# Gates of the last two up-projection batches on VectorE instead of TensorE

## The reference, cut to what matters

```python
x = x + xattn(layernorm(x), ctx)                  # (4, 512, 1024); stages a to c of the kernel
z = layernorm(x)                                  # stages d and e
logits = einsum('bsh,he->bse', z, gate_w)         # gate_w: (1024, 8)
routing_weights, _ = top_k(logits, 2)
h = relu(einsum('bsh,hi->bsi', z, up_w)) ** 2     # up_w: (1024, 2048)
shared_out = einsum('bsi,ih->bsh', h, down_w)
x_latent = einsum('bsh,hl->bsl', z, fc1_w)        # fc1_w: (1024, 512)
moe_out = (x_latent @ expert_w) * sum(routing_weights)
y = layernorm(shared_out + moe_out @ fc2_w, gamma, beta)
out = x + y
```

## Time and profile before

| | |
|---|---|
| median of 3 runs | 2098.47 us |
| the profiled execution | 2098.85 us |
| its span, first to last instruction | 2097.1 us |
| TensorE busy | 2076.1 us, 99% |
| VectorE, ScalarE, GpSimd busy | 805.5, 693.4, 754.7 us |
| mean granted TensorE clock | 0.997 |

### The profile page before, as it was taken

How to read it: one execution, slowest core, us unless ns; L and a number is a source line. 1 busy time by engine, 2 the same in 40 slices (tenths; PEclk the granted TensorE clock), 3 DMA queues, 4 the chain that set the end, 5 groups by cost and what they waited for, 6 DMA issues and landing times.

```text
span 2097.1 us, 30206 instructions
## 1 busy us (share of the span) xinstructions
PE 2076.1 (99%) x9532; PEld 1732.2 (83%) x9532; DVE 805.5 (38%) x1418; ACT 693.4 (33%) x1206; POOL 754.7 (36%) x616
## 2 busy tenths in 40 slices
PE   8999999999999999999999999999999999999998
PEld 7888888888888888888888878787878888888886
DVE  4221312178888888831121412313231332222223
ACT  5121111167777777741111223112123311111111
POOL 2533030147777777662112343010024422222221
PEclk9999999999999999999999999999999999999999
DMA  5743433635655655534347554252433622222222
GB/s 194 255 171 141 146 124 107 183 83 146 158 149 148 161 153 142 129 117 150 130 157 198 210 156 145 105 156 104 136 99 134 207 91 84 90 90 86 85 76 67
DMA packets 302750, 286.29 MB, mean 137 GB/s; under 512 B 146896, under 2 KB 214480, under 8 KB 301776
## 3 DMA queue, kind: packets, MB, share of 16 engines
q1 hardware_dynamic: 188128, 196.58, 29.9%
q10 hardware_dynamic: 114544, 88.76, 14.9%
HBM read 184.32 MB, written 100.68 MB: 136 GB/s over the span
## 4 chain that ended last, share of the span: by engine, by line
PE 97%; DVE 1%; ACT 1%; DMA 0%; issue 0%; POOL 0%; SPq 0%; DVEq 0%; POOLq 0%; ACTq 0%
PE psum L118 30%; PE psum L119 30%; PE psum L120 30%; PE psum L985 3%; PE psum L1031 1%; PE psum L1032 1%; PE psum L1012 1%; PE psum L1013 1%; PE psum L1697 0%; PE psum L1696 0%; DMA staging<-in_wqkv 0%; PE psum L232 0%; DVE small L181 0%; DMA staging<-in_ctx 0%; DVE operands L353 0%
## 5 line engine op out<-in xcount | busy, mean ns | idle before, releaser
L118 PE MATMUL psum<-operands 128*128 128x512 f32 (+3 forms) x2888 | 1113.7, 386 | 9.7 <-DVE operands L353 9.4
L119 PE MATMUL psum<-operands 128*128 128x512 f32 (+3 forms) x2888 | 1111.9, 385 | 0.0
L120 PE MATMUL psum<-operands 128*128 128x512 f32 (+3 forms) x2888 | 1109.2, 384 | 0.0
L118 PEld LDWEIGHTS psum<-operands 128*128 128x128 f32 (+1 forms) x2888 | 544.6, 189 | 109.0 <-DVE operands L353 9.3
L120 PEld LDWEIGHTS psum<-operands 128*128 128x128 f32 (+1 forms) x2888 | 545.0, 189 | 105.9
L119 PEld LDWEIGHTS psum<-operands 128*128 128x128 f32 (+1 forms) x2888 | 545.6, 189 | 94.6
L1276 POOL TENSOR_TENSOR operands<-staging,operands 128x512 fp32r<-128x512 f32 x92 | 118.7, 1301 | 349.8 <-ACT operands L1271 349.3
L1157 DVE TENSOR_REDUCE small<-psum 128x1 fp32r<-128x576 f32 x256 | 192.9, 754 | 89.8 <-PE psum L985 89.7
L1935 POOL TENSOR_TENSOR operands<-operands 128x640 fp32r<-128x640 f32 x64 | 100.8, 1577 | 319.1 <-ACT operands L1930 319.1
L905 POOL TENSOR_TENSOR operands<-staging,operands 128x512 fp32r<-128x512 f32 x128 | 164.5, 1293 | 34.4 <-ACT operands L1079 25.6
L1786 DVE TENSOR_TENSOR staging<-staging 128x512 f32<-128x512 f32 x64 | 46.6, 748 | 322.6 <-ACT staging L1744 321.8
(11 more groups left out here) (111 smaller groups left out, 1284.7 us busy)
## 6 DMA issues: line engine op xcount, KB each, us to landing
h_scratch<-staging ACTq DMA_DIRECT2D x80, 256.0 KB, 2.3
operands<-h_scratch SPq DMA_DIRECT2D x64, 320.0 KB, 3.1
operands<-recip_scratch SPq DMA_DIRECT2D x64, 192.0 KB, 4.3
o_scratch<-staging SPq DMA_DIRECT2D x64, 192.0 KB, 5.0
operands<-o_scratch SPq DMA_DIRECT2D x64, 192.0 KB, 2.8
operands<-q_hi_scratch ACTq DMA_DIRECT2D x14, 768.0 KB, 5.9
operands<-q_lo_scratch ACTq DMA_DIRECT2D x14, 768.0 KB, 6.2
staging<-in_x SPq DMA_DIRECT2D x20, 512.0 KB, 3.6
```

What stands on the lines that cost most here:

```text
L118: e.matmul(o, lh, rh, start=first, stop=False)
L119: e.matmul(o, lh, rl, start=False, stop=False)
L120: return e.matmul(o, ll, rh, start=False, stop=last)
```

## The change

The gates of batches 2 and 3 are made by VectorE, in the bodies of batches 1 and 2, while z lies in rows in `XN2`. A copy of the gate weights, transposed (8 experts x 1024), is put in memory as `g_d`. SP loads sixteen rows of 512 of it for each of the two batches, each spread over all 128 partitions, into two buffers that take the place of `GW` once TensorE's gates of batches 0 and 1 are done; twelve of these loads stand ahead of job f3's, four ahead of f0's. For each row VectorE issues four `tensor_tensor_reduce` (one for each tile of tokens): z's half row times the spread row into a PSUM bank that is free (one bank in group 0, two later), and the sum into one column of `g_acc`. Rows 0 to 2 stand after group 0, 3 to 7 after group 1, 8 to 12 after group 2, 13 to 15 after group 3, and then the copy of the sums and the two largest.

To have z early enough, the load of x1, the root and the norm of the next batch go to the front of the body, on ScalarE ahead of group 0's eviction and on VectorE ahead of group 0's squares; the store of z goes from group 2 to group 1. Jobs now stand ahead of the block loads, and after group 3 ScalarE waits for the copy of the sums before it loads blocks over z. TensorE's loop makes gates in batches 0 and 1 alone. VectorE's two middle bodies are written out instead of a loop.

```diff
+        def d_gate_row_in(e, b, i):
+            if i == 0:
+                e.wait_ge(*past(g_rl[0], 16))
+                e.sem_inc(idle, 1)
+                e.wait_ge(*past(d_gm, 2))
+                e.sem_inc(idle, 1)
+            e.wait_ge(*past(g_use, b * (ST * GR) + ST * (i - 1 - GR)))
+            e.sem_inc(idle, 1)
+            e.dma_start(raw(g_row[i % 2]), g_d[i * NB:(i + 1) * NB].partition_broadcast(P)).then_inc(g_rl[i % 2], 16)
+
+        def d_gate_row(e, b, i, banks):
+            x, h = i // 2, i % 2
+            n = ((b - 1) * GR + i) * ST
+            e.wait_ge(*past(g_rl[i % 2], 16 * ((b - 1) * NE + x) + (32 if h == 0 else 16)))
+            for t in range(ST):
+                e.wait_ge(*past(g_use, n + t + 1 - banks))
+                e.tensor_tensor_reduce(PS[:, 7 - (t + 1) % banks, :], XN2[:, t, h * NB:(h + 1) * NB], raw(g_row[i % 2]), 1.0, 0.0, ALU.mult, ALU.add,
+                                       g_acc[:, t, h * NE + x:h * NE + x + 1]).then_inc(g_use, 1)
 d_sp_eng:
+                        if not isinstance(b, int) and at == 3:
+                            for i in range(12):
+                                d_gate_row_in(e, b, i)
+                        if not isinstance(b, int) and at == 4:
+                            for i in range(12, GR):
+                                d_gate_row_in(e, b, i)
                         job_load(e, j, n_before + m)
 d_pe:
-            with e.Fori(0, B - 1) as b:
+            with e.Fori(0, 2) as b:
+                body(b, True)
+            with e.Fori(2, B) as b:
                 body(b, False)
-            body(B - 1, True)
 d_act:
+                if not last and not first:
+                    d_load(e, x1_d, b + 1)
                 run(-1, b)
+                if not last and not first:
+                    d_sqrt(e, b + 1)
...
-                    if g == 0 and not last and not first:
-                        d_load(e, x1_d, b + 1)
-                    if g == 2 and not last and not first:
+                    if g == 1 and not last and not first:
                         d_z_out(e, b + 1)
+                    run(g, b)
+                    if g == 3 and not last and not first:
+                        e.wait_ge(*past(d_gc, b * GC + (GC + 1)))
                     if g in (3, 4) and not last and not first:
                         d_blocks_in(e, b + 1, g - 3)
-                    run(g, b)
-                    if g == 1 and not last and not first:
-                        d_sqrt(e, b + 1)
 d_dve:
+                to_gate = not last and not first
+                if to_gate:
+                    d_norm(e, b + 1)
+                    e.wait_ge(*past(d_zn, b + 2))
...
-                    if g == 0:
+                    if g == 0 and b < 2:
...
+                    if to_gate and g < 4:
+                        for i in range((0, 3, 8, 13)[g], (3, 8, 13, GR)[g]):
+                            d_gate_row(e, b, i, 2 if g else 1)
+                    if to_gate and g == 3:
+                        e.wait_ge(*past(g_use, b * (ST * GR)))
+                        link(e.tensor_copy(gsum, g_acc), b + 1, 1)
+                        top2(b + 1, gsum)
```

More of the change, by code:

```diff
@@ L3, with xattn_ffn_kernel @@
 from contextlib import ExitStack
-def xattn_ffn_kernel(nc, x, xt, ctx, wqkv, wo, gate_w, up_w, down_w, fc1_w, fc2_w, expert_w, gamma, beta, out):
+def xattn_ffn_kernel(nc, x, xt, ctx, wqkv, wo, gate_w, gate_t, up_w, down_w, fc1_w, fc2_w, expert_w, gamma, beta, out):
     f32 = mybir.dt.float32
@@ L54, in xattn_ffn_kernel @@
     z_d = dram("z_scratch", (S, D))
+    g_d = dram("gate_scratch", (NE * D,))
     m_d = nc.dram_tensor("moments_scratch", (2 * S,), f32, kind="Internal").ap()
@@ L144, in norm_z @@
             sq = sem(f"{tag}_sqrt")
-            cp, cx = sem(f"{tag}_copied"), sem(f"{tag}_centered")
+            cp, cx = (sem(f"{tag}_copied"), sem(f"{tag}_centered")) if tiles else (None, None)
             own = 2 if tiles else 0
@@ L1650, in jobs_of @@
             return JOBS_MID, b * N_MID + (M_MID - N_MID)
+        GR = 2 * NE
+        g_row = [MM[:, 22 * SLOT + r * NB:22 * SLOT + (r + 1) * NB] for r in range(2)]
+        g_acc = sm[:, 0:ST * GR].rearrange("p (t e) -> p t e", t=ST)
+        g_rl = [sem(f"gate_row_loaded{r}") for r in range(2)]
+        g_use = sem("gate_row_used", ST + 1)
+        def d_gate_row_in(e, b, i):
[15 more added lines that the diff above has]
+                                       g_acc[:, t, h * NE + x:h * NE + x + 1]).then_inc(g_use, 1)
         def d_sp_eng(e):
@@ L1676, in d_pe, with body @@
         def d_pe(e):
-            def body(b, last):
+            def body(b, gates):
                 def wait_bank(g, c):
@@ L1702, in gate @@
                         e.transpose(PS[:, 6, 0:P], gTs, ident[:]).then_inc(d_gt, 1)
-                mm_groups(e, b, D_GROUPS, d_zl, wait_bank, job_slot, d_acc, slot_ready, gate, d_fr)
+                mm_groups(e, b, D_GROUPS, d_zl, wait_bank, job_slot, d_acc, slot_ready, gate if gates else None, d_fr)
             e.wait_ge(*past(cc_x1, B * ST - 1))
-            with e.Fori(0, B - 1) as b:
+            with e.Fori(0, 2) as b:
+                body(b, True)
+            with e.Fori(2, B) as b:
                 body(b, False)
-            body(B - 1, True)
         def d_act(e):
@@ L1795, in body, with link, top2 @@
                         m.then_inc(d_gl, 1)
-                    if g == 1:
+                    def link(ins, b, q):
+                        ins.then_inc(d_gc, 1)
+                        e.wait_ge(*past(d_gc, b * GC + q))
+                        e.sem_inc(idle, 1)
+                    def top2(b, sums):
+                        link(e.tensor_tensor(g8, sums[:, :, 0:NE], sums[:, :, NE:2 * NE], ALU.add), b, 2)
+                        for t in range(ST):
+                            link(e.max(gtop[:, t, :], g8[:, t, :]), b, 3 + t)
+                        link(e.tensor_tensor(rw[:, b * ST:(b + 1) * ST], gtop[:, :, 0], gtop[:, :, 1], ALU.add), b, GC)
+                    if g == 1 and b < 2:
                         e.wait_ge(*past(d_gt, b + 1))
                         e.sem_inc(idle, 1)
[L1799 to L1814, removed]
+                        link(e.tensor_copy(gsum, PS[:, 6, 0:P].rearrange("p (t e) -> p t e", t=ST)[:, :, 0:2 * NE]), b, 1)
+                        top2(b, gsum)
+                    if to_gate and g < 4:
[5 more added lines that the diff above has]
+                        top2(b + 1, gsum)
             e.wait_ge(*past(d_gw, 16))
@@ L1823, in d_dve @@
             body(0, False, True)
-            with e.Fori(1, B - 1) as b:
+            for b in range(1, B - 1):
                 body(b, False)
@@ L2109, in _ @@
             e.sem_inc(idle, 1)
+            e.dma_start(g_d, gate_t).then_inc(g_rl[0], 16)
             e.dma_start(graw, gate_w.rearrange("(k p) e -> p k e", p=P)).then_inc(d_gw, 16)
@@ L2188 @@
         "gate_w": inputs[_F + "gate_w"],
+        "gate_t": np.asarray(inputs[_F + "gate_w"]).T.reshape(-1),
         "up_w": in_chunks(inputs[_F + "up_w"]),
```

## The result

The changed kernel takes 2107.6 us (median of six runs, 2106.49 to 2111.75) against 2098.52 before: a ratio of 1.0047, 95% interval 1.0037 to 1.0058. It is 9.1 us slower. The forecast was +4.3 us (2103.2 for a profiled execution), in a range of 2091 to 2119, with 0.53 on slower: right in its direction, at half the size.

What follows compares the result with a forecast made beforehand. TensorE was taken to bound the kernel. Batch 1 +6.1, batch 2 +1.7 and batch 3 -3.9 us gave +3.9, plus 0.4 for stops: +4.3 on 2098.85, so 2103.2 us, range 2091 to 2119.

Steps and rivals of the forecast that it cites:

- The mechanism: Batches 1 and 2: VectorE's rows delay the copied sums, so block loads come late and TensorE stalls at the next batch.
- The gates' slots: TensorE, batches 2 and 3: gate matmuls and transposition removed, 3.87 us a batch, -7.7 us in all.
- a chain of fixed length behind the copied sums: ScalarE's block loads, evictions and job f0, then VectorE's turns: next batch starts 33.5 + 0.1 us after the copy.
- The steps costed at nothing: Gate-weight copy, SP's load order, unrolled VectorE bodies and TensorE's other loop bound: no time added.
- Price of a row instruction: VectorE's multiply-and-sum, 64 a batch: 0.70 us apart, 0.86 in group 0; bounds 0.60 and 0.9.
- rival 4: VectorE row instructions at half rate, 1.14 us apart: +56 us and more, 2160; chance 0.04.
- GpSimd: Low parts of jobs f2 and f3 run beside VectorE's rows: 1.2 us lost for each, 0 to 2.5.
- The loads: Row loads feeding VectorE: waits of 0.3 to 0.6 us a group, plus 1.5 behind the z store in group 1.
- rival 2: Row loads set the pace at 4.5 us each: +14 us, 2117; chance given only within 0.49 for larger losses.
- I add 0.4 for the two longer stops: TensorE's starts of batches 2 and 3: pipe fill and later evictions of chunks 1 and 2 paid again, 0.4 us.
- The forecast's terms for z in batch 2: Load of x1 issued 2.8 us after the batch's start; z ends at +21.8.
- Rival 1: VectorE's rows fit, copies at 79.1 and 75.25 us just met, whole 7.7 us gain stays: 2091.1; chance 0.21 with near cases.

Runs made afterwards that it cites:

- experiment 3: The change with one of the four instructions of each gate row (tile 0 alone), all row loads kept: 2090.36 us against 2098.26, ratio 0.9961.
- experiment 6: The change with eight more row instructions ahead of the last row in batches 1 and 2: 2120.49 us against 2098.26, ratio 1.0106.
- experiment 7: The change with the second sixteen block loads issued by SP instead of ScalarE: 2093.49 us against 2098.4, ratio 0.9975.
- experiment 1: The kernel before, with block loads issued after groups 4 and 5 instead of 3 and 4: 2116.86 us against 2098.4, ratio 1.0084.
- experiment 2: The change without rows, row loads and wait for sums, all gates on TensorE, new order kept: 2097.97 us against 2098.4, ratio 0.9998.
- experiment 4: The change with two row loads for a batch instead of sixteen, all 64 instructions kept: 2093.26 us against 2098.4, ratio 0.9975.
- experiment 8: The change with block loads split between SP (first half) and ScalarE (second), in three variants; medians from 2093.54 to 2096.11 us.
- the kernel with f0 moved: The change with first half of block loads on SP, second on ScalarE, and job f0 moved behind group 6: 2093.54 us, ratio 0.9978.
- experiment 5: The change with GpSimd's low parts of job f3 held back until the sums are copied: 2105.1 us against 2098.26, ratio 1.0035.
- the first kernel of experiment 8: The change with SP issuing the first sixteen block loads, ScalarE the second after group 4: 2094.09 us, ratio 0.9985; run again, 2096.11 us, 0.9984.

## Why the prediction was right, and where it was off

**The mechanism was right, the size was not.** The loss is twice the one forecast. The gates' slots are worth 7.7 us (experiment 3: 7.9). The end of the batch hangs on a chain of fixed length behind the copied sums: forecast 33.6 us, measured 33.2 (1397.16 to 1430.34) and 34.0; experiments 6 (more delay, same growth) and 7 (chain cut, gain back) show it from both sides, and experiment 1 shows it without the rows. The steps costed at nothing cost nothing (experiment 2). Batch 1 came out to the tenth, 118.8 us, in part by luck: rows in group 0 were cheaper than said, GpSimd and the loads dearer.

**Price of a row instruction.** Said 0.70, and 0.86 where each waits for the one before; measured 0.65 (1352.74 to 1353.39) and 0.79. The read-out of the sum is an instruction of its own, 0.14 us, but the next product starts with it (both at 1353.39), and the spacing is 0.05 over a plain product's 0.60. Half rate (rival 4) is out: 0.65 a piece with both inputs f32 in SBUF.

**GpSimd, mis-sized.** Said 1.2 us for each job, from squares that met it at their edges; measured 2.1 for each of the four pairs: two instructions of 1.77 to 1.83 us where the others take 0.73. GpSimd's first pair beside the rows, and a pair of the kernel before while VectorE was idle:
```profile
1370.42 3.40 POOL L1277 TENSOR_TENSOR operands<-staging,operands 128x512 fp32r<-128x512 f32 x2 [44.06 <-ACT operands L1272]
```
```profile
1394.58 2.54 POOL L1276 TENSOR_TENSOR operands<-staging,operands 128x512 fp32r<-128x512 f32 x2 [21.95 <-ACT operands L1271]
```
The Trainium skill (SBUF — State Buffer, "SBUF: two separate sides") calls the shared port an exclusive lock. By the forecast's full price for it that was 2.5 a job, and the trace is nearer to that than to my 1.2. But GpSimd loses as well, 3.40 us instead of 2.54 (2.98 in the last of the four pairs).

**The loads, mis-sized in batch 2.** ScalarE issues the 2 MB store of z of each batch:
```profile
1350.41 0.41 ACTq L1338 DMA_DIRECT2D z_scratch<-staging  x1
...
1468.04 0.41 ACTq L1338 DMA_DIRECT2D z_scratch<-staging  x1
```
and the chain that ended last has the row load that meets it, from issue to landing:
```profile
1354.93 4.45 DMA operands<-gate_scratch
...
1470.14 6.40 DMA operands<-gate_scratch
```
VectorE waited 1.97 and 3.93 us for these two, where 1.5 was said. The load was issued 4.5 us behind the store in batch 1 and 2.1 in batch 2, whose rows of group 1 have no top-2 ahead of them, and landed 9.0 and 8.5 us after the store's issue. Nearer behind the store it took longer, and the forecast used one price for both. All load waits were 3.9 and 5.9 us, against 3.0 forecast for each: 3.8 us too much, about a quarter of the 14 that rival 2 put on top; 2.9 of the 3.8 are in batch 2.

**The clock, missed.** The step that failed is "I add 0.4 for the two longer stops": it has no term for the lower clock after a stop. That cost 1.9 us in batch 3, which comes straight on top, and 2.8 in batch 2. The latter doesn't add to the time by itself, as that batch's end was set by VectorE's chain; it delays group 1's eviction there, for which VectorE waited 1.0 us.

**The sum.** Batch 2 is 3.6 us longer than forecast. By the table, 0.9 of this came ahead of group 1's rows (the load of x1 took 8.6 us instead of 7.8, and the 1.0 us for the clock, less cheaper rows), 1.5 in group 1 (the load behind the store), 0.3 and 0.5 in groups 2 and 3 (GpSimd, less cheaper rows) and 0.4 behind the copy. The forecast's terms for z in batch 2, 2.8 + 7.8 + 10.7, give 21.3 and not the 21.8 it wrote; z ended at 22.5. As measured: batch 1 +6.1 as forecast, batch 2 +5.3 instead of +1.7 (118.0 less 112.7), batch 3 -2.0 instead of -3.9 (gates gone, clock 1.9 lost): 9.4 us in the profiled executions from batch 1 on, against 9.1 by the medians. Rival 1 needed the copy at 79.1 and 75.25 after each start; it came at 85.6 and 84.0.

## What to carry to other kernels

When work moves from the engine that bounds to an idle one, look not at its share of busy time but at what is queued behind the new wait: here 45 us of work fitted beside 34 in a batch of 113 (VectorE was busy for 80), but stood ahead of a chain of 33 us, of which ScalarE's issues of 32 block loads were 18. Before taking such a change back, cut that chain: another engine's queue for half of the issues turned +9.1 us into -5. And price a stop of TensorE above its own length where traces show the lower clock behind stops of that length: here 1.9 and 2.8 us behind stops of 6.2 and 5.7.

## What the runs showed of the hardware that was not expected

- TensorE's clock after a stop, in these runs: waits of 0.9 (experiment 4), 1.1 (experiment 8, the kernel with f0 moved) and 2.2 us (experiment 7) were followed by no matmul at the lower clock; one of 2.5 us (experiment 8) and all from 4.5 to 6.8 us (the change, experiments 1, 5, 6) by 8 to 14 matmuls at 0.43 us instead of 0.23, 1.6 to 2.9 us lost. There is no order by length in this: 2.5 us lost after a stop of 4.5, and 1.6 after one of 5.6, both in experiment 6.
- A DMA issue of ScalarE for these block loads takes its queue about 0.5 us (8.4 us for the first sixteen, 9.8 for the second, 1409.00 to 1418.76), so 32 small loads are 18 us in which ScalarE does almost nothing else. The pace varies: in the first kernel of experiment 8 it is 0.70 us each, as ScalarE's timeline has it, and in experiment 7 0.56, with SP issuing sixteen at the same pace beside it. Why it varies is open:
```profile
1403.80 10.44 ACTq L1346 DMA_DIRECT2D staging<-z_scratch  x15
```
```profile
1398.50 8.89 ACTq L1346 DMA_DIRECT2D staging<-z_scratch  x16
```
- A multiply-and-sum of 512 f32 on VectorE comes at 0.65 us with its read-out, at 0.79 where it waits for the one before.
